# Running register offsets for the sums, and job results kept until the last row scatter

## The chip, the cores and the metric

One core of one Trainium2 chip runs the whole program. The metric is device time in microseconds, the median of three runs. TensorE is PE, VectorE is DVE, ScalarE is ACT, GpSimd is POOL and SyncE is SP.

## The reference

The program takes a graph of 6250 nodes with 256 features and 100000 edges, which come sorted by destination (`dst`). With `xn` the layer norm of `x`, it computes

```
h  = segment_sum((xn @ W + b)[src], dst) / max(degree, 1)
m  = linear attention over all nodes: elu+1 features of q and k, 8 heads, then wo
x1 = x + h + m
out = x1 + expert(layernorm(x1))
```

The expert part is a mixture of 8 experts (256 to 1024 to 256, ReLU): each node goes to its best expert, a place in that expert's queue is given in node order, places past 977 get nothing, and the result is weighted with the gate's probability. All is float32 in and out.

## The kernel before

**Tiles and groups.** The 6250 nodes are 49 tiles of 128 (NT = 49). The edges are 196 groups of 4 x 128 (G = 4, a group's number is `f`). A tile's sum is a few groups: 29 for the first tile and 3 or 4 for the late ones; neighbouring tiles share a group, so there are 244 additions of a group to a tile.

**Gathers (POOL).** `gather` issues for each group four indirect DMAs (line 591) that fetch 128 rows of `table` each into one of RQ = 7 slots of a ring (`gathered`). When the group before has landed, `report` (line 571) counts `relayed` up; that is what PE waits for. POOL's loop holds BODY = 14 groups. At every second group `events` looks whether tiles are due: when `f - LAG` has passed the last group of the tile after next, `event(t)` runs.

**Events (POOL).** `event(t)` waits until VectorE has placed tile t's nodes (`row_ok`), scatters the tile's rows of x1 to the experts' queues in DRAM (`rows`, line 544), and, from the eighth tile on (T0 = 8), calls `finish`: it waits for one earlier job scatter to have landed (`fin_sc`), frees its buffer (`fin_free`), waits for the next job's result (`fin_ok`) and scatters it to `out` (line 531). The buffer is one of FB = 4 (`fin`, `jtok`) and is picked by a tree of branches (`pick`). The queue of POOL is in order, so what stands behind an event waits for it.

**Sums (PE).** `add(f, final)` waits for `relayed` and `oh_ready`, then multiplies four one-hot matrices (written by VectorE, OQ = 4 slots) with the group's four gathered blocks into the bank `pA` (line 920). The slots are computed from the group's number and the pair's number (`n % OQ`, `(f % RQ) * G + j`). The last matmul of a non-final add frees the ring slot (`slots`); the final one counts `agg_done`. `sum_start` begins a tile, `sum_rest` runs what is left in a loop (line 954).

**Steps.** Each engine runs `step(t)` for tile t. On PE: project tile t-1's sums (line 1018), count places, `expert` of job t-9 (second layer, line 1041), `hidden` of job t-8 (first layer, line 1050), turn sums and rows, then the sum of tile t+1. A job is 128 places of one expert's queue; job numbers run from 0. SP loads for each step the job's rows (behind `scat_done`), then the weights (behind `h0_ps`, `h1_ps`), then the bias `b2r` (behind `y_sb`), in that order on one queue. On VectorE the step ends with `post` of job t-9: it takes PE's result (line 1547), waits for a free buffer (`fin_free`), replaces values that are not finite (lines 1552 to 1556) and writes the token numbers (line 1558) and the sum with the row (line 1559). `base[:, t, :]` is tile t's attention part plus x; `node_out(t)` reads it long before job t is done.

**Tail.** After step 50 the remaining jobs run in loops whose number comes from the counts: here jobs 42 to 53. POOL's tail loop calls `finish` for each result that is left. The order of all this is written by hand.

Of the kernel before, what the change touches and what calls it, by code (L numbers as in the profile page):

```python
# [25 lines left out]
G = 4  # L26
# [39 lines left out]
PLANNED = J0 + LEAD  # L66
JB = 4
# [13 lines left out]
def gps_block(nc, x, src, dst, gnn_w, gnn_b, wq, bq, wk, bk, wv, bv, wo, bo,  # L81
# [8 lines left out]
    with ExitStack() as ctx:  # L90
# [38 lines left out]
        x0 = FIRST * G * D  # L129
        gathered = shared[:, 0:RING * D].bitcast(F16).rearrange("p (s d) -> p s d", d=2 * D)  # L130
# [71 lines left out]
        onehot = sb("onehot", [P, OQ, G, P], F16)  # L202
        sel_f = onehot[:, :, :, :].rearrange("p a b c -> p (a b c)").bitcast(F32)
# [14 lines left out]
        jtok = sb("jtok", [P, FB], I32)  # L218
# [256 lines left out]
        def _(g):  # L475
# [47 lines left out]
            def finish(j):  # L523

                g.wait_ge(S["fin_sc"], j * 16 + 16)
                g.sem_inc(S["fin_free"], 1)
                g.wait_ge(S["fin_ok"], j + 1)
                hold(g, "pool_hold")

                def send(b):  # L530
                    g.indirect_dma_start(out[:, :], bass.IndirectOffsetOnAxis(ap=jtok[:, b:b + 1], axis=0),  # L531
                                         fin[:, b, :], None,
                                         bounds_check=N - 1, oob_is_err=False).then_inc(S["fin_sc"], 16)
                pick((g.snap(j % FB), 0), FB, send)

            def event(t, done_r):

                g.wait_ge(S["scat_done"], t * 16 + 16)
                g.sem_inc(S["row_free"], 1)
                g.wait_ge(S["row_ok"], t + 1)  # L540
                hold(g, "pool_hold")

                def send(b):
                    g.indirect_dma_start(rows[:, :], bass.IndirectOffsetOnAxis(ap=row_at[:, b:b + 1], axis=0), rows_sb[:, b, :], None,  # L544
                                         bounds_check=ROWS - 1, oob_is_err=False).then_inc(S["scat_done"], 16)
                pick((g.snap(t % RB), 0), RB, send)
                with g.If(T0 - 1 < t):
                    finish(g.snap(done_r))
                    g.reg_add(done_r, done_r, 1)
                    g.sem_inc(S["pool_hold"], 1)  # L550

# [7 lines left out]
            def events(tile, tend, done_r, f):  # L559


                with g.While(lambda: g.snap(tend) < f - LAG):
                    event(g.snap(tile), done_r)
# [14 lines left out]
            def gather(i, q, tile=None, tend=None, done_r=None):  # L578
# [4 lines left out]
                if q % 2 == 0 and not (first and q < RQ):  # L583
                    events(tile, tend, done_r, f)
# [21 lines left out]
            with g.register("tile_no") as tile, g.register("tile_end") as tend, g.register("jobs_done") as done_r:  # L606
                g.reg_mov(tile, 0)
                g.reg_mov(done_r, 0)
                load_end(tend, BEHIND)
                for q in range(FIRST, BODY):  # L610
                    gather(0, q, tile, tend, done_r)
                with g.Fori(1, turns) as i:
                    for q in range(BODY):
                        gather(i, q, tile, tend, done_r)
# [204 lines left out]
        def _(pe):  # L819
# [87 lines left out]
            with pe.register("held") as at_r, pe.register("pair") as pair_r, pe.register("now") as now_r, pe.register("last") as last_r:  # L907
                pe.reg_mov(at_r, 0)
                pe.reg_mov(pair_r, 1)
# [18 lines left out]
                def sum_start(w):  # L928

                    lo = pe.snap(w // PACK)  # L930
                    pe.reg_mov(now_r, lo)
                    pe.reg_mov(last_r, lo + w % PACK - 1)
                    at_ = pe.snap(at_r)
                    with pe.If(at_ < lo):
                        with pe.Fori(at_, lo) as f:
                            pe.wait_ge(S["relayed"], f + 1)
# [231 lines left out]
        def _(v):  # L1168
# [180 lines left out]
            with v.register("pair_v") as pair_r, v.register("first") as first_r, v.register("early_end") as mid_r, v.register("end") as end_r:  # L1349
# [189 lines left out]
                def post(j):  # L1539
# [10 lines left out]
                    v.wait_ge(S["fin_free"], j + 1)  # L1550
                    v.sem_inc(S["dve_hold"], 1)
# [6 lines left out]
                    v.tensor_copy(jtok[:, bass.ds(j % FB, 1)], jrow[:, j % JB, C_TOK:C_TOK + 1].bitcast(I32))  # L1558
                    v.tensor_tensor(fin[:, j % FB, :], yc, jrow[:, j % JB, 0:D], ALU.add).then_inc(S["fin_ok"], 1)
# [62 lines left out]
                v.sem_inc(S["fin_free"], FB - 1)  # L1622
# [30 lines left out]
                with v.Fori(0, n) as i:  # L1653
                    post(i + (J0 - 1))
                    plan(i + (PLANNED + 2), 1.0)
                end = v.value_load(last_job, min_val=J0, max_val=J0 + NX * JOBS)
                post(end)
# [27 lines left out]
```

## Time and profile before

| | |
|---|---|
| median of three runs | 1451.4 us (1449.21 to 1453.46) |
| the profiled execution | 1447.8 us, span 1446.1 us |
| PE busy | 1135.0 us (78%) |
| POOL busy | 920.9 us (64%) |
| DVE busy | 809.9 us (56%) |
| ACT busy | 558.2 us (39%) |
| gathers (line 591) | 784, 766.4 us busy, 317.8 us idle before them |
| job scatters (line 531) | 54, 55.6 us busy, 107.2 us idle before them |
| row scatters (line 544) | 49, 50.1 us busy, 63.4 us idle before them |

Busy time is a share of the whole span; the span has stretches with different limits (the gathers end at 1289 us, after which POOL has only scatters). Idle time "before" a group is the time in which its engine stood still just ahead of it, and the arrow names what ended that. "issue" means that the profile shows nothing that was waited for: mostly the engine's own register, branch and semaphore steps, which do not count as busy. The queue of an engine's sequencer carries a q (POOLq, PEldq).

### The profile page before, as it was taken

To read this page: it belongs to the slowest core of one execution; us is meant where nothing else is said; L and a number is where in the kernel's file an instruction comes from. 1 tells how busy PE (TensorE), PEld (TensorE's weight loads), DVE (VectorE), ACT (ScalarE), POOL (GpSimd) and SP (SyncE) were. 2 spreads that over 40 slices of the span, in tenths; PEclk is the share of its full clock that TensorE was granted. 3 is DMA by queue.
4 is the path that set the end of the run, shared out by engine and by line. 5 is a ranking of instruction groups with operands and counts; after the bars stand their busy time and mean duration, and the time that the engine had idled before them with its cause. 6 is when DMAs were issued, how large, how long until landed. Compare 5 with 4: busy or idle time off the path is not lost.

```text
span 1446.1 us, 33945 instructions
## 1 busy us (share of the span) xinstructions
PE 1135.0 (78%) x5961; PEld 805.2 (56%) x5962; DVE 809.9 (56%) x2755; ACT 558.2 (39%) x1433; POOL 920.9 (64%) x967
## 2 busy tenths in 40 slices
PE   3769876857786788888676888787888788888896
PEld 2456553535454555665454565555555566667885
DVE  6754432747567666675544555464655566666443
ACT  4822221323233233343333444353454444545342
POOL 4646776777777767767677676776766666751111
PEclk9579997978889779999978999899999999999998
DMA  7593334454455456454545545555555555555552
GB/s 218 200 300 90 103 103 132 124 147 132 135 151 150 150 163 194 143 170 149 165 135 178 158 155 164 175 174 164 178 174 164 189 191 170 171 163 161 162 182 84
DMA packets 143378, 231.82 MB, mean 160 GB/s; under 512 B 29824, under 2 KB 87329, under 8 KB 143248
## 3 DMA queue, kind: packets, MB, share of 16 engines
q0 software_dynamic: 42896, 115.65, 26.5%
q1 hardware_dynamic: 99118, 114.27, 25.2%
q14 instruction: 109, 0.89, 0.2%
q10 hardware_dynamic: 1234, 0.66, 0.2%
q8 instruction: 21, 0.34, 0.1%
HBM read 197.40 MB, written 35.08 MB: 161 GB/s over the span
## 4 chain that ended last, share of the span: by engine, by line
PE 29%; issue 26%; POOL 23%; DVE 7%; DMA 4%; POOLq 4%; ACT 3%; DVEq 1%; SPq 1%; ACTq 0%; PEldq 0%
POOL shared L591 22%; PE pA L920 6%; PE pH L1050 6%; PE pY L1041 6%; DMA shared<-table,idx 2%; DVE shared L1417 2%; PE pQ L964 2%; PE pT L972 2%; PE pX L1018 1%; PE pD L978 1%; DMA shared<-in_L_ffn_b_dram 1%; PE pD L979 1%; PE pH L900 1%; DVE shared L1423 1%; DVEq L1365 1%
## 5 line engine op out<-in xcount | busy, mean ns | idle before, releaser
L591 POOL DMA_INDIRECT shared<-table,idx x784 | 766.4, 978 | 317.8 <-issue 271.8
L920 PE MATMUL pA<-shared,onehot 128*128 x976 | 286.3, 405 | 148.1 <-POOLq L571 86.0
L920 PEld LDWEIGHTS pA<-shared,onehot 128*128 x976 | 92.4, 99 | 329.2 <-issue 254.0
L1357 DVE TENSOR_TENSOR onehot<-tile_iota,dst_t 128x512 f32 x244 | 160.1, 694 | 103.7 <-PE pA L920 66.4
L1041 PE MATMUL pY<-w2s,shared 128*128 x864 | 203.2, 389 | 11.2 <-issue 9.5
L1050 PE MATMUL pH<-shared 128*128 128x128 f32 x1728 | 204.8, 277 | 8.5 <-DMA shared<-in_L_ffn_w_dram 8.5
L1050 PEld LDWEIGHTS pH<-shared 128*128 128x128 f32 x1728 | 203.9, 194 | 12.3 <-DMA shared<-in_L_ffn_w_dram 9.7
L1041 PEld LDWEIGHTS pY<-w2s,shared 128*128 128x128 f32 x864 | 162.0, 193 | 35.9 <-issue 15.2
L771 ACT ACTIVATE shared<-pH,b1s 128x128 f32<-128x128 f32 x432 | 122.3, 370 | 89.3 <-PE pH L1050 82.2
L706 ACT ACTIVATE shared<-pA 128x512 f32<-128x512 f32 x49 | 29.3, 597 | 281.2 <-PE pA L920 281.2
L1399 DVE TENSOR_SCALAR tile_iota<-tile_iota 128x128 f32<-128x128 f32 x48 | 12.5, 261 | 213.2 <-PE pA L920 213.2
L531 POOL DMA_INDIRECT out_dram<-shared,jtok x54 | 55.6, 1029 | 107.2 <-issue 107.2
L1417 DVE RECIPROCAL shared<-shared 128x256 f32<-128x256 f32 x49 | 85.9, 1753 | 37.1 <-ACT shared L721 33.9
L544 POOL DMA_INDIRECT rows<-rows_sb,row_at x49 | 50.1, 1023 | 63.4 <-issue 63.4
L972 PE MATMUL pT<-shared,ks 128*128 128x128 f32 x196 | 39.2, 330 | 58.0 <-ACT shared L763 30.1
L1018 PE MATMUL pX<-wgs,shared 128*128 128x264 f32 x196 | 66.1, 468 | 11.8 <-issue 10.8
L972 PEld LDWEIGHTS pT<-shared,ks 128*128 128x128 f32 x196 | 30.3, 221 | 80.1 <-issue 80.1
L714 ACT ACTIVATE shared<-pQ,bqs 128x128 f32<-128x128 f32 x196 | 55.8, 367 | 29.4 <-PE pQ L964 29.4
L721 ACT ACTIVATE shared<-pT,eps 128x256 f32<-128x256 f32 x49 | 23.0, 468 | 106.9 <-PE pT L972 99.0
L737 ACT ACT_TABLE_LOAD x49 | 62.9, 1283 | 0.9
L964 PE MATMUL pQ<-xts,wqs 128*128 (+1 forms) x392 | 63.1, 314 | 0.0
L743 ACT ACT_TABLE_LOAD x49 | 62.9, 1283 | 0.2
(248 smaller groups left out, 1651.0 us busy)
## 6 DMA issues: line engine op xcount, KB each, us to landing
shared<-in_L_ffn_w_dram SPq DMA_DIRECT2D x108, 512.0 KB
shared<-table,idx POOLq DMA_INDIRECT x784
w2s<-in_L_ffn_w_dram SPq DMA_DIRECT2D x8, 1024.0 KB, 6.9
rows<-rows_sb SPq DMA_DIRECT2D x7, 1040.0 KB, 14.7
shared<-rows SPq DMA_DIRECT2D x54, 130.0 KB
shared<-in_L_ffn_b_dram SPq DMA_DIRECT2D x54, 128.0 KB
shared<-in_x_dram SPq DMA_DIRECT2D x12, 512.0 KB, 8.3
table<-w2s SPq DMA_DIRECT2D x12, 512.0 KB, 4.0
```

Of the source, the lines that this page charges most:

```text
L591: g.indirect_dma_start(gathered[:, s * G + j, :], None, table[:, :], bass.IndirectOffsetOnAxis(ap=idx[:, q * G + j:q * G + j + 1], axis=0) ...
L737: a.activation(sd[:, 0:1], sc[:, 1:2], ACT.Sqrt, bias=eps[:, 0:1]).then_inc(S["sd_ok"], 1)
L743: a.activation(lg[:, 1, :], lg[:, 0, :], ACT.Exp, bias=sc[:, 4:5], scale=-1.0, accum_out=sc[:, 5:6]).then_inc(S["ex_ok"], 1)
L771: ins = a.activation(hs[:, h * FC // 2 + c, :], ph[:, c * P:(c + 1) * P], ACT.Relu, bias=b1s[:, bass.ds(e * FC + h * FC // 2 + c, 1)])
L920: m = pe.matmul(pA[:, :], onehot[:, n % OQ, j, :], gathered[:, (f % RQ) * G + j, :], start=False, stop=final and j == G - 1)
L964: ins = pe.matmul(pQ[:, m * P:(m + 1) * P], wqs[:, k, m * P:(m + 1) * P], xts[:, bass.ds(i, 1), k, :].rearrange("p t n -> p (t n)"), start ...
L972: ins = pe.matmul(pT[:, m * P:(m + 1) * P], ks[:, m, :], qf[:, m * P:(m + 1) * P], start=True, stop=True)
L1018: ins = pe.matmul(pX[:, 0:GW], st[:, k * P:(k + 1) * P], wgs[:, k, :], start=(k == 0), stop=(k == DK - 1))
L1041: ins = pe.matmul(pY[:, 0:D], hs[:, c, :], w2s[:, bass.ds(e * FC * D + c * D, D)], start=(c == 0), stop=(c == FC - 1))
L1050: ins = pe.matmul((pH0, pH1)[h][:, c * P:(c + 1) * P], w1b[:, h, k, c * P:(c + 1) * P], xjt[:, k * P:(k + 1) * P], start=(k == 0), stop=(k ...
L1357: v.tensor_tensor(onehot[:, n % OQ, :, :], tile_iota[:, :].rearrange("p (a n) -> p a n", a=1).broadcast_to([P, G, P]), dst_t[:, bass.ds(ch ...
L1417: k(v.reciprocal(dn, dn))
```

## The change

Two edits. On PE, the ring offset (`got_r`) and the one-hot offset (`one_r`) are kept in registers: each `add` steps them and takes the modulo, and the two waits stand directly ahead of these steps, against registers that already hold the value to wait for (group numbers and pair numbers run one higher than before). The matmuls read flat views (`got_of`, `one_of`) at the register's offset.

On POOL and VectorE, the results of jobs 0 to 43 (KEPT = 44) are written into `base[:, j, :]` and their token numbers into 44 columns of `jtok`, without a wait for a free buffer; `event` no longer calls `finish`. After the last event POOL scatters these 44 one after the other, each behind `fin_ok`, and then runs `finish` for the remaining jobs, whose first waits until all 44 have landed.

```diff
+KEPT = J0 + LEAD - 2
+        got_of = [shared[:, 0:RING * D].bitcast(F16)[:, j * 2 * D:(RING - G + j + 1) * 2 * D] for j in range(G)]
+        one_of = [onehot[:, :, :, :].rearrange("p a b c -> p (a b c)")[:, j * P:(OQ * G - G + j + 1) * P] for j in range(G)]
-        jtok = sb("jtok", [P, FB], I32)
+        jtok = sb("jtok", [P, KEPT + FB], I32)
-            def finish(j):
+            def finish(r):
-                g.wait_ge(S["fin_sc"], j * 16 + 16)
+                g.wait_ge(S["fin_sc"], r * 16 + (KEPT + 1) * 16)
                 g.sem_inc(S["fin_free"], 1)
-                g.wait_ge(S["fin_ok"], j + 1)
+                g.wait_ge(S["fin_ok"], r + KEPT + 1)
...
+            def send_kept(j):
+                g.wait_ge(S["fin_ok"], j + 1)
+                g.indirect_dma_start(out[:, :], bass.IndirectOffsetOnAxis(ap=jtok[:, j:j + 1], axis=0), base[:, j, :], None,
+                                     bounds_check=N - 1, oob_is_err=False).then_inc(S["fin_sc"], 16)
...
-                with g.If(T0 - 1 < t):
-                    finish(g.snap(done_r))
-                    g.reg_add(done_r, done_r, 1)
-                    g.sem_inc(S["pool_hold"], 1)
...
                 with g.Fori(g.snap(tile), NT) as t:
-                    event(t, done_r)
+                    event(t)
+            for j in range(KEPT):
+                send_kept(j)
             g.wait_ge(S["tail_ok"], 1)
-            end = g.value_load(last_job, min_val=J0, max_val=J0 + NX * JOBS)
-            with g.Fori(NT - T0, end + 1) as j:
-                finish(j)
+            end = g.value_load(last_job, min_val=J0 + LEAD - 1, max_val=J0 + NX * JOBS)
+            with g.Fori(0, end - (KEPT - 1)) as r:
+                finish(r)
...
                 def add(f, final):
-                    n = pe.snap(pair_r)
-                    pe.wait_ge(S["relayed"], f + 1)
-                    pe.sem_inc(S["pe_hold"], 1)
-                    pe.wait_ge(S["oh_ready"], n + 1)
+                    pe.wait_ge(S["relayed"], f)
+                    pe.reg_add(got_r, got_r, G * 2 * D)
+                    pe.reg_alu(got_r, got_r, RING * 2 * D, ALU.python_mod)
+                    pe.wait_ge(S["oh_ready"], pair_r)
+                    pe.reg_add(one_r, one_r, G * P)
+                    pe.reg_alu(one_r, one_r, OQ * G * P, ALU.python_mod)
+                    got = pe.snap(got_r, min_val=0, max_val=(RING - G) * 2 * D)
+                    one = pe.snap(one_r, min_val=0, max_val=(OQ - 1) * G * P)
                     for j in range(G):
-                        m = pe.matmul(pA[:, :], onehot[:, n % OQ, j, :], gathered[:, (f % RQ) * G + j, :], start=False,
+                        m = pe.matmul(pA[:, :], one_of[j][:, bass.ds(one, P)], got_of[j][:, bass.ds(got, 2 * D)], start=False,
                                       stop=final and j == G - 1)
...
-                    pe.reg_mov(now_r, lo)
-                    pe.reg_mov(last_r, lo + w % PACK - 1)
+                    pe.reg_mov(now_r, lo + 1)
+                    pe.reg_mov(last_r, lo + w % PACK)
+                    pe.reg_mov(got_r, (lo + (RQ - 1)) % RQ * (G * 2 * D))
...
-                def post(j):
+                def post(j, r=None):
...
-                    v.wait_ge(S["fin_free"], j + 1)
-                    v.sem_inc(S["dve_hold"], 1)
+                    if r is not None:
+                        v.wait_ge(S["fin_free"], j + 1)
+                        v.sem_inc(S["dve_hold"], 1)
...
-                    v.tensor_copy(jtok[:, bass.ds(j % FB, 1)], jrow[:, j % JB, C_TOK:C_TOK + 1].bitcast(I32))
-                    v.tensor_tensor(fin[:, j % FB, :], yc, jrow[:, j % JB, 0:D], ALU.add).then_inc(S["fin_ok"], 1)
+                    at_ = j if r is None else r % FB + KEPT
+                    done = base[:, j, :] if r is None else fin[:, r % FB, :]
+                    v.tensor_copy(jtok[:, bass.ds(at_, 1)], jrow[:, j % JB, C_TOK:C_TOK + 1].bitcast(I32))
+                    v.tensor_tensor(done, yc, jrow[:, j % JB, 0:D], ALU.add).then_inc(S["fin_ok"], 1)
...
-                v.sem_inc(S["fin_free"], FB - 1)
+                v.sem_inc(S["fin_free"], KEPT + FB - 1)
```

VectorE's tail loop passes `r`, the number of the job behind the kept ones, to `post`, and runs its first two jobs outside the loop.

## Rows read from the trace of the kernel before

**Rows 1.** The page, the chain that ended last, share of the span by engine.

```profile
PE 29%; issue 26%; POOL 23%; DVE 7%; DMA 4%; POOLq 4%; ACT 3%; DVEq 1%; SPq 1%; ACTq 0%; PEldq 0%
```

**Rows 2.** Groups of POOL, 640 to 925 us: count, busy, mean ns, idle before.

```profile
L591 POOL DMA_INDIRECT shared<-table,idx x175 | 170.3, 973 | 69.9 <-issue 64.7 <-PE pA L920 2.8 <-DMA shared<-table,idx 2.4
L531 POOL DMA_INDIRECT out_dram<-shared,jtok x13 | 14.4, 1105 | 5.9 <-issue 5.9
```

**Rows 3.** The same groups of POOL, 925 to 1289 us.

```profile
L591 POOL DMA_INDIRECT shared<-table,idx x209 | 204.8, 980 | 85.9 <-issue 78.1 <-PE pA L920 5.0 <-DMA shared<-table,idx 1.8
...
L531 POOL DMA_INDIRECT out_dram<-shared,jtok x22 | 22.4, 1018 | 11.2 <-issue 11.2
```

**Rows 4.** Groups of PE, 640 to 925 us.

```profile
L920 PE MATMUL pA<-shared,onehot 128*128 x224 | 72.2, 437 | 57.1 <-POOLq L571 41.5 <-issue 15.0
```

**Rows 5.** Groups of PE, 925 to 1298 us.

```profile
L920 PE MATMUL pA<-shared,onehot 128*128 x304 | 86.9, 382 | 42.8 <-issue 31.8 <-POOLq L571 9.7
L1050 PE MATMUL pH<-shared 128*128 128x128 f32 x704 | 85.2, 281 | 8.5 <-DMA shared<-in_L_ffn_w_dram 8.5
```

**Rows 6.** Timeline of PE, a late step: start us, us, instruction, [idle before].

```profile
1152.65 1.15 PE L920 MATMUL pA<-shared,onehot 128*128 x4
1154.48 1.14 PE L920 MATMUL pA<-shared,onehot 128*128 x4 [0.68 <-issue]
...
1167.99 0.39 PE L920 MATMUL pA<-shared,onehot 128*128 x1
```

**Rows 7.** Timeline of POOL around four places.

```profile
704.42 1.50 POOL L531 DMA_INDIRECT out_dram<-shared,jtok  x1 [0.63 <-issue]
...
721.67 0.94 POOL L591 DMA_INDIRECT shared<-table,idx  x1 [5.06 <-issue]
...
781.21 1.02 POOL L544 DMA_INDIRECT rows<-rows_sb,row_at  x1 [0.30 <-issue]
782.54 1.00 POOL L531 DMA_INDIRECT out_dram<-shared,jtok  x1 [0.30 <-issue]
783.84 0.99 POOL L591 DMA_INDIRECT shared<-table,idx  x1 [0.30 <-issue]
...
808.48 1.00 POOL L531 DMA_INDIRECT out_dram<-shared,jtok  x1 [0.69 <-issue]
811.10 0.98 POOL L591 DMA_INDIRECT shared<-table,idx  x1 [1.61 <-PE pA L920]
```

**Rows 8.** Steps of PE's sequencer by line: duration ns min/median/max, first, last.

```profile
L917 PEldq EVENT_SEMAPHORE  x244: 51/51/51, 112.5 to 1311.0; - x122
...
L918 PEldq ALU_OP  x244: 36/36/45, 112.6 to 1311.2; - x122
...
L920 PEldq FUSED_REGOPS  x1220: 51/74/154, 112.7 to 1312.1; - x175
...
L920 PEldq ALU_OP  x732: 32/32/32, 113.3 to 1312.3; - x183
...
L954 PEldq FUSED_REGOPS  x117: 47/47/58, 286.3 to 1309.1; - x117
```

**Rows 9.** Timeline of POOL, the last row scatter.

```profile
1337.33 0.98 POOL L544 DMA_INDIRECT rows<-rows_sb,row_at  x1 [6.15 <-issue]
```

**Rows 10.** Timeline of VectorE in the tail, jobs 47 and 48.

```profile
1390.11 0.29 DVE L1552 TENSOR_SCALAR finite<-shared 128x256 int32<-128x256 f32 x1 [0.26 <-DVE shared L1547]
...
1393.57 0.14 DVE L1537 CAST planw<-pout 1x1 f32 x1
1396.61 0.48 DVE L1547 SCALAR_TENSOR_TENSOR shared<-pY,shared 128x256 f32<-128x256 f32 x1 [2.90 <-ACT shared L757]
```

**Rows 11.** The chain that ended last, in order of time: its last piece.

```profile
1431.37 2.13 DMA out_dram<-shared,jtok
```

**Rows 12.** Busy time by stretch: PE, PEld, DVE, ACT, POOL, clock, DMA share, GB/s.

```profile
1339.00:1396.00 57.00, 52.40 (x358) 48.54 (x357) 24.85 (x104) 24.39 (x77) 7.86 (x8) 1.00 0.57 173
```

**Rows 13.** The page, DMA queues: packets, MB, share of 16 engines' span.

```profile
q0 software_dynamic: 42896, 115.65, 26.5%
```

More of the change, by code:

```diff
@@ L557, in load_end, with events @@
                 g.reg_add(reg, reg, -1)
-            def events(tile, tend, done_r, f):
+            def events(tile, tend, f):
                 with g.While(lambda: g.snap(tend) < f - LAG):
-                    event(g.snap(tile), done_r)
+                    event(g.snap(tile))
                     g.reg_add(tile, tile, 1)
@@ L576, in copy_idx, with gather @@
                 g.tensor_copy(idx[:, o:o + HALF], src_t[:, bass.ds((i % TURNS) * IDX + o, HALF)]).then_inc(S["idx_ok"], 1)
-            def gather(i, q, tile=None, tend=None, done_r=None):
+            def gather(i, q, tile=None, tend=None):
                 s = q % RQ
@@ L583, in gather @@
                 if q % 2 == 0 and not (first and q < RQ):
-                    events(tile, tend, done_r, f)
+                    events(tile, tend, f)
                 if q % RQ == 0:
@@ L905, in _ @@
             pe.sem_inc(S["oh_slots"], OQ - 1)
-            with pe.register("held") as at_r, pe.register("pair") as pair_r, pe.register("now") as now_r, pe.register("last") as last_r:
-                pe.reg_mov(at_r, 0)
-                pe.reg_mov(pair_r, 1)
+            with pe.register("held") as at_r, pe.register("pair") as pair_r, pe.register("now") as now_r, pe.register("last") as last_r, \
+                 pe.register("one") as one_r, pe.register("got") as got_r:
+                pe.reg_mov(at_r, 1)
+                pe.reg_mov(pair_r, 2)
+                pe.reg_mov(one_r, 0)
                 def load_span(t):
@@ L930, in sum_start @@
                     lo = pe.snap(w // PACK)
-                    pe.reg_mov(now_r, lo)
-                    pe.reg_mov(last_r, lo + w % PACK - 1)
+                    pe.reg_mov(now_r, lo + 1)
+                    pe.reg_mov(last_r, lo + w % PACK)
+                    pe.reg_mov(got_r, (lo + (RQ - 1)) % RQ * (G * 2 * D))
                     at_ = pe.snap(at_r)
-                    with pe.If(at_ < lo):
-                        with pe.Fori(at_, lo) as f:
-                            pe.wait_ge(S["relayed"], f + 1)
+                    with pe.If(at_ < lo + 1):
+                        with pe.Fori(at_, lo + 1) as f:
+                            pe.wait_ge(S["relayed"], f)
                             pe.sem_inc(S["slots"], 1)
@@ L1652, in _ @@
                 plan(PLANNED + 1, 1.0)
-                with v.Fori(0, n) as i:
+                for i in range(LEAD - 1):
                     post(i + (J0 - 1))
                     plan(i + (PLANNED + 2), 1.0)
-                end = v.value_load(last_job, min_val=J0, max_val=J0 + NX * JOBS)
-                post(end)
+                with v.Fori(0, n - (LEAD - 1)) as r:
+                    post(r + KEPT, r)
+                    plan(r + (PLANNED + LEAD + 1), 1.0)
+                end = v.value_load(last_job, min_val=J0 + LEAD - 1, max_val=J0 + NX * JOBS)
+                post(end, v.snap(end - KEPT))
 _INS = ["x", "src", "dst", "L0_gnn_W", "L0_gnn_b", "L0_mix_wq", "L0_mix_bq", "L0_mix_wk", "L0_mix_bk", "L0_mix_wv", "L0_mix_bv",
```

13 lines of the change are left out of this document (6 added, 7 removed).

## The prediction

> **What bounds the kernel now.** The chain that ended last comes first: PE and "issue" have 29% and 26% of it, POOL 23% [rows 1], so no single engine bounds the whole span and the stretches have to be read apart. The first job scatter (line 531) runs at 640 us and the last gather (line 591) ends at 1289, so I cut the span there and once more at 925, and ask each piece for two views: POOL's groups and PE's groups.
>
> From 640 to 925 the reader is to see a POOL that never rests: 175 gathers busy 170.3 us and idle 69.9 us before them, of which 175 x 0.30 = 52.5 us is the fixed gap that stands before every gather; with 13 job scatters (14.4 + 5.9 us) POOL is full [rows 2]. PE meanwhile stands 41.5 us at its sums (line 920) for line 571, the relay that tells it that a gather has landed [rows 4]. POOL is the bound there.
>
> From 925 to 1289 POOL is nearly as full (209 gathers 204.8 + 85.9 us, 22 job scatters 22.4 + 11.2 us) [rows 3], but PE's waits have shrunk to 9.7 us for the relay and 8.5 us for weights at line 1050 [rows 5]. Here a step is PE's own time: three adds and the expert work repeat every 1167.99 - 1152.65 = 15.3 us, an add every 1.83 us, of which 1.15 us is its four matmuls and 0.68 us idle put down to "issue", that is, PE's own register steps [rows 6]. The weight wait belongs to POOL as well: SP loads weights behind a row load that waits for the row scatter, and that scatter stands in POOL's queue behind the gathers.
>
> After 1289 there are no gathers and POOL is mostly idle; jobs set the pace.
>
> **Job scatters out of the events.** 54 job scatters exist; 41 ran inside events, 13 + 22 of them between 640 and 1289. With the change none runs there. First piece: 14.4 + 5.9 = 20.3 us of POOL go directly [rows 2]. Then the register steps: behind an event without backlog the scatter follows after 0.30 and the next gather after 0.30, in another the scatter after 0.69 and the gather after 1.61 (808.48, 811.10) [rows 7]: the event's branches outlast the queued gathers. The gathers' idle above 0.30 is 69.9 - 52.5 = 17.4 us, of which 4.8 is one long pause that stands behind no event (721.67, 5.06) [rows 7]; of the other 12.6 I give half, 6 us, to the job scatter's branches (bounds 0 and 12.6). Sum 26 us, and PE can follow, since it waits 41.5 us for POOL there [rows 4].
>
> Second piece: 22.4 + 11.2 = 33.6 us, and half of 85.9 - 62.7 = 23.2 us, together 45 us of POOL time [rows 3]. But PE waits only 9.7 + 8.5 = 18.2 us there [rows 5], so POOL's relief alone is worth at most 18; I take two thirds, 12, since the pauses of the kind of 721.67 stay.
>
> **Offsets in PE registers.** An add now issues about 12 register steps: the wait (line 917, 51 ns), line 918 (36 ns), in the loop one at line 954 (47 ns), five FUSED_REGOPS and three ALU_OP at line 920 (1220 and 732 over 244 adds), one of these up to 154 ns, and the pair's increment [rows 8]. 1.83 us over 12 is 0.15 us a step with what surrounds it. The change drops the three short ones (the waits ride on the offsets' steps) and adds two offset steps with a modulo; the eight address steps of the eight operands stay, but from a plain register each can be nearer the 32 ns of the ALU_OP than the 74 ns of the median FUSED_REGOPS. Net one step and some shortening: I take 0.2 us less per add. Bounds: 0.68 us less (the whole gap gone), or 0.2 us more (two steps of the longest kind, 154 ns, in place of the short ones). Nothing that the trace shows measures a register modulo alone, so both ends stay in the range.
>
> In the second piece 304 / 4 = 76 adds x 0.2 = 15 us, all on the path [rows 5]. In the first piece POOL is late, not PE: nothing. Before 640 neither edit is worth anything: no job scatters, and the sums there run at the gathers' pace. Queued behind PE's new waiting step are only its own matmuls, which need that wait anyway.
>
> Late next in the first piece is still POOL, in the second PE. Main part: 26 + 12 + 15 = 53 us.
>
> **The kept scatters in the tail.** 44 results are kept; their scatters, straight-line, start behind the last row scatter (1337.33, 0.98 us) [rows 9], at 1338.6 on the old clock, at 0.98 + 0.30 each. POOL's row queue is done by then; what is queued behind them is the ten remaining jobs' scatters. The fourth of these jobs (number 47) needs a buffer that is freed only when all 44 have landed. The last starts at 1338.6 + 43 x 1.28 = 1393.6 and lands 2.1 us behind its start, as the chain's last job scatter does [rows 11]: 1395.8. Before, job 47's post went on at 1390.11, and VectorE then idled 2.90 us before the next job's first step at 1396.61 [rows 10]; so it can be released at 1393.0 without harm, and the wait costs 1395.8 - 1393.0 = 2.8 us, once.
>
> The transfers cost too. 44 x 131 KB = 5.8 MB; the queue of indirect transfers took 26.5% of 16 engines' span for 115.65 MB [rows 13], 3.3 us per MB, so 19 us in a 57 us window whose share was 0.57 [rows 12]: 0.91. There is room, but the weights come in bursts and share the engines. Bounds 0 and 19 us; the two costs overlap (later jobs make the buffer wait vanish), and I take 5 us for both. The Trainium skill (DMA: Bandwidth & Descriptors, SWDGE vs HWDGE vs iDMA) says that each DMA engine takes turns between the queues of GpSimd's DMAs and of the others: by that rule a weight burst in the window would always be stretched, and the cost would lie nearer 10 us than 5; no row here shows the two at full load together.
>
> VectorE's side is free: the posts of kept jobs lose a wait on a free buffer, and the row they write has already been read.
>
> **Sum.** The profiled execution took 1447.8 us (span 1446.1). 1447.8 - 53 + 5 = 1400. The median of the three runs lies 3.6 us above it, so 1403 us is forecast. The likeliest case's own range is 1390 to 1419.
>
> **Rivals.**
> Adds no shorter (the modulo steps eat what the waits gave): the second piece keeps 12 us only, 1447.8 - 38 + 5 = 1415, as a median 1418. For it: the same number of operand steps. Against: three steps gone.
> Adds much shorter (0.43 us): 76 x 0.43 + 12 = 45 us, where POOL's 45 us cap it; 26 + 45 - 5 = 66 us, 1385.
> PE takes over in the first piece as well, and only half of POOL's relief pays: 13 + 15 - 5 = 23 us, 1428. Against it: the 41.5 us of waits.
> Scatters starved in the tail: one of 1.50 us is seen where VectorE writes one-hots (704.42) [rows 7]. At 1.80 each the last lands at 1338.6 + 43 x 1.80 + 2.1 = 1418, 25 us too late: 53 - 25 = 28 us, 1423. [...] Against it: the job scatters of the tail took 0.98 us beside the same posts.
> Slower than before: the kept chain alone eats the gain. It decides where job 47 is released at 1393.0 + 53 = 1446, which is 2.45 us a scatter; at 2.6 it ends 6 us above before, 1458. No scatter in the trace took so long.
> The change does nothing (POOL's time goes into longer pauses before the gathers): 1451.
>
> **Chances.** Forecast 0.60; adds no shorter 0.13; much shorter 0.09; PE takes over 0.07; starved 0.05; slower 0.03; nothing 0.03. A measurement of this kernel tells 0.3%, some 4 us, from no change. Faster 0.93, same 0.04, slower 0.03. The range 1386 to 1430 leaves out much shorter adds (just), the slower case and no change, 0.15 in all.
>
> **What would show it.** No line of job scatters on POOL before the last row scatter, then 44 at a spacing of 1.28 us; the gathers' end some 45 us earlier; the spacing of adds in a late step 1.63 us and the step 14.7 us; in the tail job 47 released about 58 us behind the last row scatter. If gathers end early and PE's steps still repeat every 15.3 us, the adds' term was wrong; if the time from the last row scatter to the end grows by more than 10 us, the tail's was.

## The result, and the profile after

The changed kernel takes 1436.4 us (median of four runs, 1432.7 to 1437.2) against 1450.3 us of the kernel before (1448.5 to 1453.5): ratio 0.9902, 95% interval 0.9879 to 0.9924. It is faster, by 14 us where 47 were forecast, and outside the range given. Its profiled execution took 1432.74 us, span 1430.9, so 15 us of the sum's 48 arrived. A profile shows one execution, and some here lie up to 8 us beside the median of their kernel; whole times are therefore compared by medians, and profiles are read for where time goes.

Groups of POOL in the changed kernel over the same gathers as before, that is from 649 to 922 us (before 640 to 925) and from 922 to the last at 1266. Columns: line, engine, operation, count, busy us, mean ns, idle us before and what ended it. L595 is the gather, L553 the row scatter. They answer to [rows 2, 3].

```profile
L595 POOL DMA_INDIRECT shared<-table,idx x177 | 172.3, 973 | 71.0 <-issue 69.1 <-DMA shared<-table,idx 1.2 <-DVE row_at L1537 0.3
L553 POOL DMA_INDIRECT rows<-rows_sb,row_at x14 | 14.7, 1053 | 12.9 <-issue 12.9
...
L595 POOL DMA_INDIRECT shared<-table,idx x208 | 205.1, 986 | 86.0 <-issue 80.8 <-PE pA L931 3.4 <-DMA shared<-table,idx 1.5
L553 POOL DMA_INDIRECT rows<-rows_sb,row_at x21 | 21.4, 1017 | 29.1 <-issue 27.1 <-DVE row_at L1537 1.7 <-PE pA L931 0.3
```

The job scatters are gone, as forecast. The gathers' idle is not a microsecond smaller (71.0 and 86.0, before 69.9 and 85.9), where I had taken 6 and 11.6 us off it, and that of the row scatters is larger (12.9 and 29.1 us; before 10.5 and 15.0). The last gather ends at 1266 us, 23 earlier than before, where 45 were expected.

Groups of PE over the same two pieces, the second to 1291 (L931 the adds, L1062 the first layer of a job); they answer to [rows 4, 5].

```profile
L931 PE MATMUL pA<-shared,onehot 128*128 x224 | 65.0, 421 | 53.7 <-POOLq L575 42.2 <-issue 11.3
...
L1062 PE MATMUL pH<-shared 128*128 128x128 f32 x736 | 93.4, 289 | 11.9 <-DMA shared<-in_L_ffn_w_dram 11.9
L931 PE MATMUL pA<-shared,onehot 128*128 x316 | 80.8, 377 | 28.0 <-issue 22.7 <-POOLq L575 3.7
```

PE still waits 42.2 us for relays in the first piece. In the second, its own register steps ("issue") fell from 31.8 to 22.7 us, but the wait for weights rose from 8.5 to 11.9.

The timeline of PE in a late step, answering to [rows 6]: start us, us, instruction, idle before.

```profile
1151.08 1.02 PE L931 MATMUL pA<-shared,onehot 128*128 x4
1152.57 1.02 PE L931 MATMUL pA<-shared,onehot 128*128 x4 [0.46 <-issue]
1153.95 1.02 PE L931 MATMUL pA<-shared,onehot 128*128 x4 [0.36 <-issue]
1165.48 1.02 PE L931 MATMUL pA<-shared,onehot 128*128 x4 [0.16 <-issue]
```

Adds start 1.49 and 1.38 us apart instead of 1.83 (the four matmuls take 1.02 us instead of 1.15, the gaps are 0.46 and 0.36 instead of 0.68), and the step is 1165.48 - 1151.08 = 14.4 us instead of 15.3.

The tail on POOL: the last row scatter, the first and the last kept scatter (L542), the first finish scatter (L534). It answers to [rows 9].

```profile
1315.45 0.98 POOL L553 DMA_INDIRECT rows<-rows_sb,row_at  x1 [8.08 <-issue]
1316.73 0.98 POOL L542 DMA_INDIRECT out_dram<-xts,jtok  x1 [0.30 <-issue]
...
1372.72 0.98 POOL L542 DMA_INDIRECT out_dram<-xts,jtok  x1 [0.30 <-issue]
1378.47 0.98 POOL L534 DMA_INDIRECT out_dram<-shared,jtok  x1 [4.77 <-issue]
```

And on VectorE, job 47, which waits once for a buffer (L529, POOL frees it); it answers to [rows 10].

```profile
1373.30 0.48 DVE L1559 SCALAR_TENSOR_TENSOR shared<-pY,shared 128x256 f32<-128x256 f32 x1 [3.45 <-ACT shared L762]
1377.40 0.29 DVE L1565 TENSOR_SCALAR finite<-shared 128x256 int32<-128x256 f32 x1 [3.62 <-POOLq L529]
```

The 44 kept scatters run mostly 1.28 to 1.30 us apart, for 56 us, and the buffer wait is 3.62 us where 2.8 was worked out.

**Where the 15 us came from.** I place the end of each tile's last add in both profiles and read three differences, at tile 13 (682 us before), tile 25 (931) and tile 48 (1313 before), and the tail behind tile 48. The table has them for every kernel of this study, against the first profile of the kernel before (us; negative is earlier).

```
kernel                         tile 13   tile 25   tile 48   tail
before                             0         0         0    133.4
before, second profile          -1.1      -5.6      -8.0    133.9
changed                         +6.5      -3.5     -22.0    140.2
changed, second profile         +5.1      -6.6     -26.7    140.4
adds' part alone                +3.2      +1.8      +6.2    135.0
scatters' part alone           +10.5      -2.2     -14.5    144.6
changed, no kept scatters       +9.3      -4.0     -22.5    134.1
changed, kept spread            +8.7      -3.5     -19.7    136.1
before, weights first           +0.2     -11.4     -17.3    135.7
scatters' part, weights first  +10.3     -14.5     -30.5    142.1
changed, weights first          +5.6     -19.8     -59.4    140.3
changed, relay after event      -1.7     -30.2     -66.3    143.7
all three                       -2.9     -35.5     -74.3    140.4
adds' part, weights, relay      -3.4     -26.3     -60.0    137.3
```

For the change, by its first profile: 6.5 us lost before tile 13, 10.0 gained from there to tile 25, 18.5 in the second piece, 6.8 lost in the tail: -15.2 together, the difference of the spans. The prediction's first piece begins at 640 us, though, nearer to tile 11, whose last add ends at 634 us before. Counted from there, 9.0 us were lost ahead of the first piece (forecast nothing), 12.5 gained in it (26), 18.5 in the second (27), 6.8 lost in the tail (5). A second profile moves a piece by up to 4.5 us, and in the kernel before three pieces moved the same way, 8.0 us at tile 48. So differences under 5 us in a piece, or under 8 in a column, say nothing here.

### The profile page after: what moved, and what is told of

It reads as the page before. It is cut to its first block, busy times and chain, and to the rows that moved or that the text cites. A ratio compares the mean times of both kernels' runs of the same rounds, so it can differ in the third digit from the quotient of the medians.

```text
span 1430.9 us, 32256 instructions
## 1 busy us (share of the span) xinstructions
PE 1118.1 (78%) x5961; PEld 814.7 (57%) x5962; DVE 812.7 (57%) x2755; ACT 558.9 (39%) x1433; POOL 922.6 (64%) x967
## 4 chain that ended last, share of the span: by engine, by line
issue 25%; PE 25%; POOL 23%; DVE 8%; DMA 8%; POOLq 4%; ACT 3%; DVEq 2%; SPq 2%; ACTq 0%
POOL shared L595 22%; PE pH L1062 6%; PE pY L1053 5%; PE pA L931 4%; DMA shared<-table,idx 4%; DVE shared L1429 2%; PE pH L905 2%; DMA shared<-in_L_ffn_b_dram 1%; DMA shared<-in_L_ffn_w_dram 1%; PE pT L984 1%; PE pQ L976 1%; PE pX L1030 1%; DMA rows<-rows_sb,row_at 1%; POOLq L558 1%; DVE shared L1435 1%
## 5 line engine op out<-in xcount | busy, mean ns | idle before, releaser
L595 POOL DMA_INDIRECT shared<-table,idx x784 | 768.7, 980 | 328.2 <-issue 293.3
L931 PE MATMUL pA<-shared,onehot 128*128 x976 | 266.0, 401 | 139.4 <-POOLq L575 101.5
L931 PEld LDWEIGHTS pA<-shared,onehot 128*128 x976 | 92.9, 99 | 289.6 <-issue 231.4
L1053 PE MATMUL pY<-w2s,shared 128*128 x864 | 209.2, 397 | 17.2 <-issue 13.2
L1062 PE MATMUL pH<-shared 128*128 128x128 f32 x1728 | 209.6, 281 | 12.5 <-DMA shared<-in_L_ffn_w_dram 12.5
L1062 PEld LDWEIGHTS pH<-shared 128*128 128x128 f32 x1728 | 208.3, 198 | 16.9 <-DMA shared<-in_L_ffn_w_dram 14.3
L1053 PEld LDWEIGHTS pY<-w2s,shared 128*128 128x128 f32 x864 | 166.2, 198 | 44.1 <-issue 21.9
L553 POOL DMA_INDIRECT rows<-rows_sb,row_at x49 | 51.1, 1042 | 88.9 <-issue 86.6
L1429 DVE RECIPROCAL shared<-shared 128x256 f32<-128x256 f32 x49 | 85.9, 1753 | 38.1 <-ACT shared L726 34.8
L742 ACT ACTIVATE sd<-sc,eps 128x1 f32<-128x1 f32 x49 | 14.4, 295 | 127.6 <-DVE sc L1501 127.5
L683 ACT ACTIVATE w2s<-w2s 128x256 f32<-128x256 f32 x49 | 20.4, 415 | 111.2 <-DVE w2s L1349 110.3
```

The costliest lines, as they stand in the source:

```text
L595: g.indirect_dma_start(gathered[:, s * G + j, :], None, table[:, :], bass.IndirectOffsetOnAxis(ap=idx[:, q * G + j:q * G + j + 1], axis=0) ...
L742: a.activation(sd[:, 0:1], sc[:, 1:2], ACT.Sqrt, bias=eps[:, 0:1]).then_inc(S["sd_ok"], 1)
L931: m = pe.matmul(pA[:, :], one_of[j][:, bass.ds(one, P)], got_of[j][:, bass.ds(got, 2 * D)], start=False, stop=final and j == G - 1)
L1053: ins = pe.matmul(pY[:, 0:D], hs[:, c, :], w2s[:, bass.ds(e * FC * D + c * D, D)], start=(c == 0), stop=(c == FC - 1))
L1062: ins = pe.matmul((pH0, pH1)[h][:, c * P:(c + 1) * P], w1b[:, h, k, c * P:(c + 1) * P], xjt[:, k * P:(k + 1) * P], start=(k == 0), stop=(k ...
L1429: k(v.reciprocal(dn, dn))
```

## Experiments

**1. A second profile of each kernel.** No edit.

> The changed kernel once more, for a second profile of it. Theory 'chance': the 9 us by which its profile was late at tile 10 (554 us) against the kernel before are the POOL loop's pauses as they fell in one execution; a second profile is there within 3 us of the kernel before, and the whole is 1428 to 1437. Theory 'edit': the lateness belongs to the change and is there again, 7 to 11 us at tile 10, and the whole is 1433 to 1438.

> The kernel before once more, for a second profile of it. The change's four profiles with shorter events or shorter adds were 4 to 10 us late at tile 10 (554 to 640 us). Theory 'the first profile of before was early there': this one ends tile 10 at 612 to 619, 3 to 10 us behind the first one's 609.3. Theory 'both parts of the change cost that much': it ends within 2 us of 609.3.

The changed kernel again: 1435.3 us (0.9925, 0.990 to 0.995), tile 10 late by 7.7 us. The kernel before again, one execution alone: 1440.3 us, tile 10 at 608.0, 1.3 us ahead of its first profile (609.3). So the lateness before 640 us belongs to the change; "chance" falls.

**2. Either part alone.** The change's own diff, only the hunks of PE and its two views of the tiles (`got_of`, `one_of`), or all the others.

> The adds' part of the change alone (offset registers and waits on register steps; job results scattered in the events as before). Theory 'each its own piece': nothing before 925 us, where POOL sets the pace, and 14 to 18 us between 925 and 1298, where steps of 3 adds go from 15.3 to 14.4 and of 4 from 17.2 to 15.8; tail unchanged at 133; whole 1432 to 1437. Theory 'together only': POOL, with the job scatters still in its events, holds the second piece as soon as the adds are shorter; 2 to 6 us gained there, whole 1444 to 1448. If the lateness before 640 comes from the adds' edit, tile 10 is 7 to 11 us late here, otherwise within 3.

> The scatters' part alone (results kept, scattered after the last row scatter; adds as before). Theory 'each its own piece': 10 to 13 us gained from 640 to 925, 0 to 4 from 925 to 1298, tail 6 to 7 longer; whole 1439 to 1446. The prediction as it stood: 26 and 12 gained, tail 5 longer, whole 1415 to 1420. Theory 'together only': PE with the longer adds holds the first piece too, 3 to 6 gained and the tail's 7 lost, whole 1449 to 1454. If the lateness before 640 comes from this edit, tile 10 is 7 to 11 us late here, otherwise within 3.

Adds alone: 1451.1 us, 1.0012 (0.9995 to 1.0028): nothing. Scatters alone: 1436.5 us, 0.9909 (0.9886 to 0.9932): all that the whole change gives, and none of the three theories has it: 12.7 us gained from tile 13 to 25, 12.3 behind, a tail of 144.6. Tile 10 is 4.4 us late with the adds alone and 9.5 with the scatters alone. "Together only" comes nearest for the adds, though the 2 to 6 us that it expected are not there either. Where they went is in PE's waits of the second piece of the adds' kernel (L1059 is its first layer; us in total, times, longest; this profile, 1455.7 us, is the slowest of its ten executions):

```profile
PE pH L1059 <- DMA shared<-in_L_ffn_w_dram: 22.4, 5, 6.4
PE pA L928 <- issue: 21.3, 59, 0.5
PE pA L928 <- POOLq L573: 10.6, 8, 3.2
```

"issue" fell from 31.8 to 21.3 us, as in the changed kernel; the wait for weights rose from 8.5 to 22.4. Such a wait costs more than its length. In the steps without one the 32 matmuls of the first layer take 3.73 us; behind the waits of 1.9 to 6.4 us in the adds' kernel they take 5.5 to 6.7, 11.3 us more in five steps, against 3.1 more in the kernel before. In the changed kernel, behind a wait of 2.74 us, the granted clock from 1224 to 1226 us is 0.50, the level of 1.2 GHz, and the 32 matmuls take 5.47 us. Waits and slow matmuls together went from 11.6 to 33.7 us with the adds alone: that is 22 of the some 24 us by which 76 adds are shorter. With the scatters alone the second piece gained 12.3 us, the prediction's 12, the weights' wait fell to 2.5 (4.1 with the slow matmuls), and nearly all steps are PE's own 15.3 and 17.2. Both parts together wait 11.9 for weights again, 19.4 with the slow matmuls.

**3. What holds the weights: the order of SP's loads.** In the changed kernel SP (L409 the row load, L419 the two weight loads, L389 the store of x1) near a long step:

```profile
1205.61 0.37 SPq L389 DMA_DIRECT2D out_dram<-rows_sb  x1
1216.61 0.35 SPq L409 DMA_DIRECT2D shared<-rows  x1
1217.99 1.06 SPq L419 DMA_DIRECT2D shared<-in_L_ffn_w_dram  x2
```

and the chain of waits of the same kernel there, in order of time:

```profile
1213.67 2.40 DMA rows<-rows_sb,row_at
1217.99 4.15 DMA shared<-in_L_ffn_w_dram
1222.19 5.47 PE pH L1062 x32
```

SP stands from 1205.98 to 1216.61 at the row load, which needs the row scatter that POOL issued at 1213.67; the weights behind it, which need nothing of POOL, leave at 1217.99, and PE waits for them until 1222.19. The experiment swaps the two loads in SP's step:

```
-                if rows:
-                    load_rows(t - T0 + 2, t * 16 - 16, rows == "first")
                 if weights:
                     load_weights(t - T0 + 1, weights == "first")
+                if rows:
+                    load_rows(t - T0 + 2, t * 16 - 16, rows == "first")
```

> The changed kernel with one reordering in SP's step: the next job's weight loads are issued ahead of its row load, which waits for a row scatter. Theory 'the long steps are weights held back behind a late row scatter': PE's waits for weights between 925 and 1290 (11.9 us, tiles 29, 32, 37 and 44) fall to under 3, and 5 to 10 us of the whole go with them: 1426 to 1431. Theory 'POOL's pace comes first': those waits go, but the adds then wait for relayed groups by as much; whole 1433 to 1438. Theory 'the weights' transfers themselves are slow': nothing changes, the waits stay at 9 to 13.

1402.4 us (1395.5 to 1405.5), 0.9688 (0.9671 to 0.9705): 34 us less, several times what the first theory gave. By its profile, the fastest of its four executions, the second piece gains 21 us more than in the changed kernel, where waits for weights and the slow matmuls behind them had cost 19.4, and the first piece 15 more. SP and PE's waits from 925 to 1253 us in this kernel, in two fences:

```profile
1128.01 0.36 SPq L389 DMA_DIRECT2D out_dram<-rows_sb  x1
1129.41 1.79 SPq L419 DMA_DIRECT2D shared<-in_L_ffn_w_dram  x2
1135.52 0.36 SPq L409 DMA_DIRECT2D shared<-rows  x1
```

```profile
PE pA L931 <- issue: 21.3, 58, 0.6
PE pY L1053 <- issue: 6.9, 22, 0.4
PE pX L1030 <- issue: 4.7, 22, 0.2
PE pA L931 <- POOLq L575: 2.0, 5, 0.5
```

The weights leave 1.4 us behind the store, the row load waits alone. No wait for weights is left, and relays cost 2.0 us, so from tile 25 on PE sets the pace with steps of 14.4 and 15.8 us: 39.6 us gained in the second piece, 25.4 in the first. The first piece never waited for weights; there PE's waits for relays fell from 42.2 to 26.8 us, and the likely way is through the landings. From the end of a group's fourth gather to its relay, between 640 and 925 us, the mean is 4.45 us for the 23 groups near a weight load (one issued between 1.5 us before the first gather and 2 us behind the end of the fourth) and 2.62 for the other 23 in the changed kernel; with the weights first, 3.47 and 2.62. In the kernel before the two means are 3.87 (15 groups) and 3.59 (29), so a relay can be late for other reasons; the landing itself is later near a weight load in all three kernels (last section). That weights which leave just behind a row scatter meet the gathers that follow it is my reading; no run tried it apart from the order of the loads. The rule of the Trainium skill that the prediction named (DMA: Bandwidth & Descriptors, SWDGE vs HWDGE vs iDMA), that each DMA engine takes turns between the queues, would fit these landings.

The same swap in the kernel before, and with the scatters' part alone:

> The kernel before with SP's weight loads ahead of its row load (the reordering that took 34 us off the changed kernel), neither part of the change. Theory 'the order of SP's loads cost both kernels alike': 25 to 35 us gained, whole 1413 to 1424. Theory 'the order is a limit only once the events are short and the adds fast': before, PE waited 8.5 us for weights behind 925 us; 5 to 12 gained, whole 1436 to 1444.

> The scatters' part with SP's weight loads first, adds as before: against the 1402 of the same with both parts it prices the adds' part where no weights are held back. Theory 'the adds are worth their length then': steps of 15.3 and 17.2 us against 14.4 and 15.8 for the 23 tiles behind 925 us, 20 to 26 longer, whole 1421 to 1428. The prediction's term for them: 15 longer, whole 1415 to 1419. Theory 'POOL is still the pace': 0 to 6 longer, whole 1402 to 1409.

Before: 1440.8 us, 0.9947 (0.9924 to 0.997), 8 us, the second theory. Scatters' part: 1422.6 us, 0.9811 (0.9768 to 0.9855), steps of 15.4 and 17.2 us, the first theory. Its difference to the kernel with both parts, 20 us, is what the adds are worth there. Set out by parts (medians, us; 1448 to 1450 for the kernel before in all jobs):

```
SP's order      neither   adds   scatters   both
rows first       1449     1451     1436     1436
weights first    1441      -       1423     1402
```

Where no weights are held back, the adds are worth 20 us instead of none and the scatters' part 18 instead of 12 to 13, and the change takes off 38 (some of these numbers are from different jobs). The adds with weights first and nothing else were not run.

**4. POOL's register steps behind a relay.** An event in the changed kernel (L553), with the gathers around it:

```profile
1156.72 0.95 POOL L595 DMA_INDIRECT shared<-table,idx  x1 [0.31 <-issue]
1157.97 1.28 POOL L595 DMA_INDIRECT shared<-table,idx  x1 [0.30 <-issue]
1160.12 1.02 POOL L553 DMA_INDIRECT rows<-rows_sb,row_at  x1 [0.86 <-issue]
1162.72 0.97 POOL L595 DMA_INDIRECT shared<-table,idx  x1 [1.58 <-issue]
```

0.86 + 1.58 us idle where the fixed gap is 0.30 each. In the records of POOL's sequencer the event's branches run only when the wait for the landing of the group before (`report`) is over, and by then the queued gathers nearly are too; a job scatter's own 1.3 us used to stand over part of them. The experiment calls `events` ahead of that wait:

```
-                if q % 2 == 0 and not (first and q < RQ):
-                    events(tile, tend, f)
 ...
+                if q % 2 == 1 and not (first and q < RQ):
+                    events(tile, tend, f + 1)
                 if not (first and q == 0):
                     report((s - 1) % RQ, (i * TRIPS + (q - 1) // RQ + 1) * 16 * G)
```

> The changed kernel with POOL's events moved ahead of the relay of the group before (its wait for landing), so that an event's register steps run while four gathers are still queued; the relay of that group comes some 3 us later, once in an event. Theory 'POOL's exposed register steps set the pace': the time without a gather around an event falls from 2.8 to under 1.5 us before 925 and from 3.7 to under 2.5 behind it, 36 events, and PE follows in part; 15 to 35 us gained, whole 1400 to 1421. Theory 'PE is the bound by now': the gathers run ahead and wait for free slots, whole 1430 to 1437. Theory 'a late relay costs the adds what the gathers gain': relay waits of the adds grow, whole 1434 to 1446.

1393.7 us (1391.8 to 1395.1), 0.9624 (0.9608 to 0.964): the first theory, and 6 us more than its range. Three events in a row in this kernel:

```profile
1086.14 0.95 POOL L593 DMA_INDIRECT shared<-table,idx  x1 [0.30 <-issue]
1087.39 1.02 POOL L553 DMA_INDIRECT rows<-rows_sb,row_at  x1 [0.30 <-issue]
...
1099.60 1.02 POOL L553 DMA_INDIRECT rows<-rows_sb,row_at  x1 [0.30 <-issue]
1100.93 0.97 POOL L593 DMA_INDIRECT shared<-table,idx  x1 [0.30 <-issue]
...
1111.36 1.02 POOL L553 DMA_INDIRECT rows<-rows_sb,row_at  x1 [0.30 <-issue]
1112.68 0.97 POOL L593 DMA_INDIRECT shared<-table,idx  x1 [0.30 <-issue]
```

No pause is left at these events. I add up POOL's timeline between the same two gathers in each kernel (the 397th and the 573rd: 13 events; the 573rd and the 781st: 22): what job scatters took with their 0.30, and idle time above 0.30. A stretch from one gather to the next counts whole, under the back edge if the loop's back edge lies in it (once in 14 groups its sequencer stands 2.4 to 6.6 us there, often with an event besides), else under events if it holds one, else elsewhere.

```
us                             total   job scatters   at events   back edge   elsewhere
573-397  before                287.3       18.3          7.8        13.7         5.1
         changed               271.7        0            6.7        14.2         7.3
         weights first         261.5        0            4.0        12.8         1.4
         relay after event     255.5        0            0.5         3.7         8.4
         adds, weights, relay  263.0       17.4          0.2         1.3         1.6
781-573  before                362.4       29.0         22.5        13.5         0.9
         changed               345.2        0           27.5        17.6         2.4
         weights first         320.3        0           10.5        10.3         1.8
         relay after event     315.5        0            0.2        15.3         3.7
         adds, weights, relay  330.4       29.1          0.3         1.6         1.5
```

The job scatters' 47 us did leave POOL. But the pauses did not shrink with them: they went from 26.6 to 28.2 us in the first stretch and from 37 to 47 in the second, 5 of that at events. With the weights first they are 18 and 23 us, so late landings have a part in them besides the register steps.

Also, the loss before 640 us is gone (tile 13 at -1.7). In the changed kernel the pauses at the back edge lie open there: 8.22 us without a gather up to 554.5 us against 1.90 up to 542.4 before, and over the five back edges ahead of gathers 113 to 337 19.1 us against 7.0 (6.0 in the second profile of the kernel before). Part of that is one step: the first gather behind the back edge starts 2.2 to 2.6 us behind the last step of POOL's sequencer at each back edge from gather 113 to 449, where it was 0.8 or 0.9 before. Every kernel with the scatters' part and the old place of the events has 2.17 to 5.17 us there, and every kernel with the job scatters in the events, or with the relay behind the event, 0.79 to 0.97. What makes that step longer was not tried.

**5. The tail.** First without the 44 kept scatters, then with most of them moved into POOL's idle time behind the last gather:

```
-            for j in range(KEPT):
-                send_kept(j)
```

```
+                for t in range(NT - STILL, NT):          # STILL = 5, EACH = 6
+                    with g.If(last < t + 1):
+                        event(t)
+                        ...
+                    for j in range((t - NT + STILL) * EACH, (t - NT + STILL + 1) * EACH if t < NT - 1 else KEPT):
+                        send_kept(j)
```

> The changed kernel without its 44 kept scatters (the rows of out that they would write are left out), the finish scatters as they are: the price of the kept scatters in the tail. Theory 'they cost the tail all it lost': from the last adds to the end 133 instead of 140, whole 1428 to 1431. Theory 'they cost nothing, the tail is longer for another reason' (the results of the last jobs go through a wait more): still 139 to 141, whole 1434 to 1437. Theory 'they cost more than the tail shows', because the jobs' weight and bias loads run at a quarter of the bandwidth less in it: 128 or less, whole 1424 or less.

> The changed kernel with its 44 kept scatters spread over POOL's idle time behind the last gather: 6 after each of the row scatters of tiles 44 to 47, the other 20 behind the last one; all else as changed. Theory 'the kept scatters hold the tail': with 26 us of them left behind the last row scatter instead of 56, the finish scatters keep step with the jobs again and the tail is 134 to 137 instead of 140; whole 1427 to 1433. Theory 'it is their transfers, wherever they are': tail 139 to 142, or the last steps' weights later; whole 1434 to 1438.

Without them: tail 134.1 us, the first theory; but the median, 1423.7 us (0.9824, 0.9806 to 0.9843), is 12 us below the changed kernel's in the same job and in the range of the third. So their price lies between the 6 us of the profiles' tails and 12. Spread: tail 136.1, whole 1431.2 us (0.9874, 0.985 to 0.9897), as the first theory had it. The two longest tails of the table, 144.6 and 143.7 us, are those in which job 47 waits 7.6 and 7.4 us for its buffer instead of 3.6.

**6. All three, and the scatters' part taken back.**

> The changed kernel with weight loads first, relay behind the event, and the kept scatters spread behind the last gather, all three. Theory 'PE is the bound behind 925 us, where the steps are 14.4 and 15.8 already': the relay's gain before 925 and the spread's 4 in the tail stay, the rest overlaps; end of the last adds 68 to 76 us before the first kernel's, tail 135 to 138, whole 1376 to 1388. Theory 'the gains add': 34 + 42 + 5, whole 1355 to 1362.

> The adds' part with weight loads first and relay behind the event, the job scatters in the events as before: what the scatters' part is still worth then. Theory 'POOL has room for them now': behind 925 us PE's steps stay 14.4 and 15.8, before it 5 to 15 us are lost, the tail is back at 133 to 135; whole 1388 to 1400. Theory 'POOL is the pace wherever job scatters are in the events': steps behind 925 us of 15.5 and more in the mean, whole 1405 to 1425.

All three: 1380.9 us (1378.9 to 1385.7), 0.9538 (0.9492 to 0.9584): the first theory in total (tile 48 at -74.3), not in the tail, which is 140.4 us and not 135 to 138; why is open. It is the fastest kernel here. With the job scatters back in the events: 1395.1 us, 0.9636 (0.9587 to 0.9685), in the first theory's range; steps of three adds stay at 14.4 us, but those of four take 16.0 to 17.9 instead of 15.8, and the tail is 137.3. So the scatters' part with the spread is then worth 14 us by the medians; by the profiles 9.7 in the first piece, where POOL is full, 5.1 in the second, and 3.1 lost in the tail.

## Why the prediction was wrong, step by step

**"Scatters out of the events, first piece: 20.3 + 6, and PE can follow."** This step failed, at "sum 26 us": POOL's stretch between the same two gathers became 15.6 us shorter, and PE's sums from tile 11 to 25 gained 12.5 in both profiles. The direct 20.3 was nearly right (18.3 us by gather numbers, 13 scatters; from the last gather before an event to the next one 4.33 us before, 2.89 after). What failed were the 6 us for branches, and to count only what an event loses. POOL's sequencer had gone through part of its branches, landings and back edge under the job scatters; with them gone the pauses grew by 1.6 us instead of shrinking by 6 (those at events fell by 1.1, the others rose by 2.7). The long pause at 721.67 was read as a single one; it is the loop's back edge, which comes three times in this stretch, 13.7 us in all. That PE follows was right: it waits 42.2 us for relays still.

**"Second piece: 12 of 18.2."** Right by the run with that part alone, 12.3, within the 5 us that a profile tells; the two thirds were a guess.

**"76 adds x 0.2 = 15 us, all on the path."** Wrong twice. The size: steps of three adds are 0.9 us shorter and of four 1.35, that is 0.30 to 0.34 an add, some 24 us, and 0.13 of it is in the matmuls, which the sum of register steps did not hold. And the path, the step that failed here: alone they gave nothing, on top of the scatters 6 to 8 us by the profiles and 1 by the medians; with the weights first 23.6 us in the second piece (-39.6 against -16.0) and 20 by the medians. I had written that the weight wait belongs to POOL, because SP loads weights behind a row load, and then took the adds as if that tie gave way with them. It doesn't: a faster PE needs the weights earlier, while the row scatter comes no earlier: with the adds alone the wait grew by 13.9 us and the matmuls that run slower behind it by 8.2, 22 of the 24.

**"Before 640 neither edit is worth anything."** Wrong: 6 to 9 us are lost there at tile 11, 5 to 7 still at tile 13, 3 with the adds alone and 10 with the scatters alone. With the relay behind the event nothing is lost, so it is POOL's pauses, at the back edge: 12 us more over five of them, partly because the first gather behind it starts 2.2 to 2.6 us behind the sequencer's last step instead of 0.8. What makes that step longer stays open.

**"Tail: 5."** 6.8 and 7.0 in the two profiles, 6 to 12 by the run without the kept scatters, with the spacing of 1.28 to 1.30, the release of job 47 (61.9 us behind the last row scatter, 58 forecast) and a buffer wait of 3.62 us where 2.8 was worked out. The DMA engines' share over the 57 us of the kept scatters was 0.72 (0.51 without them), where 0.91 was worked out: their transfers took some 12 us of it, not 19. Starved scatters did not come: 40 of the 44 took 0.98 to 0.99 us, the longest 1.22.

**The rivals.** The total, 1436, lies between "PE takes over in the first piece" (1428) and "nothing" (1451). The first was refuted by the relay waits; the second, "time goes into longer pauses before the gathers", named the mechanism of the 6 us that were to come from branches and did not, and had 0.03; the scatters' direct time did arrive. None named SP's order, which by the swap is worth 34 us in the changed kernel.

## What to carry to other kernels

Before a gain is credited to an engine, follow the queue of every engine that feeds it, SP's too: a load that needs nothing may stand behind one that waits, and then the wait can grow by what the faster engine saves, and the matmuls behind it run at the lower clock. When work is taken out of an in-order queue, look at what ran beneath it on that engine's sequencer; time a branch or a wait by what is queued above it. Two edits that each look idle or modest can be worth much more under another order of loads, so time them in both.

## What was not expected of the hardware

- POOL's sequencer stands 2.4 to 6.6 us at the loop's back edge, once a pass of 14 groups, in every kernel (2.45 to 5.54 in the changed one, 2.46 to 4.68 before). Behind it the next gather started 2.59 us after the last register step in the changed kernel (551.93 to 554.52) and 0.80 in the kernel before (541.64 to 542.44). An empty queue is not the reason: before gather 449 the kernel before had none queued for 4.3 us, and the step took 0.79.
- A gather group's landing takes 1.7 to 2 us longer near a weight load in the kernel before and the changed one: 3.58 against 1.92 us and 3.80 against 1.85, from the end of the fourth gather to the last record of the group's landing semaphore, for groups with at least 60 of 64 records. With the weights first it is 3.20 against 2.03.
- A wait of PE for weights costs more than its length: behind most of them PE's 32 first-layer matmuls ran partly at a granted clock of 0.50 (994 to 996 us in the adds' kernel, 1116 to 1118 and 1224 to 1226 in the changed one) and took 5.2 to 6.7 us instead of 3.73.
- The granted clock in the first 62 us of the tail is 1.00 of 2.4 GHz in both profiles of the kernel before and 0.94 in both of the changed one; in 4 us slices it falls toward the 1.2 GHz level about 20 and 36 us in, and the second layer's matmuls there take 5.19 and 5.40 us instead of 3.72 in the first profile. The kernel without kept scatters has 0.94 as well and a tail of 134.1, so the clock alone did not make the tail longer. What brings it about was not tried.
